# A fused attention and expert network on Trainium2: the order of projection's slots, its early loads, and the slot in which attention turns its probabilities

## The reference

```
x = x + cross_attention(layernorm(x), ctx)      # 16 heads of 32, RMS norm of q and k
x = x + expert_mlp(layernorm(x))                # 64 experts, 8 for each token
x = x + one_head_attention(layernorm(x), mem)
x = x + ternary_mlp(layernorm(x))
```

```
q = rms_norm(layernorm(x) @ Wq + bq) * wq ; k = rms_norm(ctx @ Wk + bk) * wk ; v = ctx @ Wv + bv
probs = softmax(q k^T / sqrt(32)) by head ; out = (probs @ v) @ Wo + bo
```

## Time and profile before

| | us |
|---|---|
| median of 3 runs | 1632.39 |
| the three runs | 1629.78, 1632.39, 1637.89 |
| profiled execution | 1634.27 |
| its span in the trace | 1632.5 |
| projection in it | 0 to 187.3 |
| attention | 187.3 to 385.5 |
| everything after | 385.5 to 1632.5 |

### The profile page before, as it was taken

The page is one execution under the profiler, slowest core; times in us unless marked ns, Lnnn a source line. Parts: engine busy times, 40 slices in busy tenths (PEclk is TensorE's granted clock), DMA queues, the critical chain, the costliest instruction groups (busy, mean ns, idle before and its releaser), DMA issues. The chain is left out here.

```text
span 1632.5 us, 37719 instructions
## 1 busy us (share of the span) xinstructions
PE 1441.0 (88%) x8673; PEld 1199.7 (73%) x8674; DVE 1035.1 (63%) x2067; ACT 900.0 (55%) x2048; POOL 618.4 (38%) x704
## 2 busy tenths in 40 slices
PE   6999799998954699999999999999971689999999
PEld 4777566666733588888888888888861478888888
DVE  4555467886678477777677666666635466766643
ACT  4544478885449266766666665666630234444442
POOL 0222267773132232233323233223317566666321
PEclk9999779999965799999999999999985789999999
DMA  5221493000152378778777777777638444444200
GB/s 199 78 78 60 163 367 134 2 2 30 57 225 99 111 257 289 269 265 284 257 260 257 273 252 261 252 235 260 223 100 279 145 147 126 129 133 141 77 13 28
DMA packets 94577, 278.16 MB, mean 170 GB/s; under 512 B 12901, under 2 KB 13030, under 8 KB 93798
## 3 DMA queue, kind: packets, MB, share of 16 engines
q1 hardware_dynamic: 68806, 196.00, 34.2%
q0 software_dynamic: 23680, 77.61, 15.8%
q10 hardware_dynamic: 2016, 3.67, 0.6%
HBM read 209.07 MB, written 76.81 MB: 175 GB/s over the span
## 5 line engine op out<-in xcount | busy, mean ns | idle before, releaser
L1132 POOL DMA_INDIRECT xg<-h_rows,idx x168 | 187.5, 1116 | 462.8 <-PE m_x L1160 453.3
L1175 PE MATMUL m_g<-wgu_high,bxTh 128*128 x660 | 236.0, 358 | 2.5 <-DVE bxTl L1248 2.4
L1175 PE MATMUL m_g<-wgu_low,bxTh 128*128 x660 | 223.5, 339 | 0.0
L1175 PE MATMUL m_g<-wgu_high,bxTl 128*128 x660 | 223.3, 338 | 0.0
L1578 PE MATMUL f_g<-x4T_high,ffn_gu 128*128 128x256 f32 x704 | 178.6, 295 | 12.3 <-DVE f_hid L1750 10.7
L1578 PE MATMUL f_g<-x4T_low,ffn_gu 128*128 128x256 f32 x704 | 172.1, 285 | 0.0
L1248 DVE TENSOR_TENSOR bxTl<-m_x,bxTh 128x512 fp32r<-128x512 f32 x166 | 114.7, 691 | 87.3 <-ACT bxTh L1317 78.3
L1010 DVE TENSOR_TENSOR wgu_low<-raw_gu,wgu_high x61 | 107.2, 1758 | 81.8 <-ACT wgu_high L1000 79.5
L1335 ACT ACTIVATE y<-m_y 128x512 f32<-128x512 f32 x164 | 98.2, 599 | 107.6 <-PE m_y L1195 89.2
L1469 POOL DMA_INDIRECT G<-y_rows,slot x128 | 132.8, 1037 | 56.2 <-issue 50.1
L573 POOL TENSOR_TENSOR prob<-prob,inv 128x512 f32<-128x512 f32 x128 | 130.4, 1039 | 59.7 <-DVE inv L524 59.6
(11 more groups left out here) (264 smaller groups left out, 3286.4 us busy)
## 6 DMA issues: line engine op xcount, KB each, us to landing
raw_gu<-in_exp_gu SPq DMA_DIRECT2D x64, 768.0 KB, 5.1
y_rows<-y SPq DMA_DIRECT2D x164, 256.0 KB
raw_d<-in_exp_d SPq DMA_DIRECT2D x64, 512.0 KB, 6.3
y_rows<-zero SPq DMA_DIRECT2D x64, 256.0 KB, 3.4
ffn_gu<-ffn_gu_words SPq DMA_DIRECT2D x1, 5632.0 KB, 22.2
raw_c<-in_ctxT SPq DMA_DIRECT2D x16, 256.0 KB, 2.9
X<-in_x SPq DMA_DIRECT2D x4, 1024.0 KB, 7.4
h_rows<-h SPq DMA_DIRECT2D x16, 256.0 KB, 2.0
```

Source lines behind the costliest of these rows:

```text
L1132: eng.indirect_dma_start(xg[:, u, :].bitcast(F32), None, h_dram, bass.IndirectOffsetOnAxis(ap=idx[half][:, u:u + 1], axis=0)).then_inc(s_g ...
L1175: m = eng.matmul(pg[u % 2][:, 0:2 * I], xT[l][:, u % 2, c, :], W.gu[r][:, buf * DC + c, :], start=c == 0 and n == 0, stop=c == DC - 1 and ...
```

## The change

In projection, PE's slot becomes k(s), v(s), turn_q(s-3), q(s-2), turn_k(s), and the last tiles are written out by hand: slot 15 is taken apart, so that k(15) stands between q(13) and q(14), and v(15) ahead of the last two turns. ACT and DVE get orders that match, with the next context tile in front of the k chain. At the start Wk and Wq go through SP in halves, Wv through ACT in halves, the rows in two DMAs (three and two rows at once) and one for `o_row`, which POOL alone waits for, on SP. ACT takes a root of a small tile first, and centring of Wq moves behind the first v bias. The DMAs of x tiles are issued one slot later in SP's order.

In attention, slot s-3 is turned in place of s-2, and ahead of the products; DVE copies heads 0, 1 and 3, ACT copies head 2, in the slot of its turn.

```diff
-        kn, qn, q_row, k_row = [scratch[i // 2][:, (i % 2) * D:(i % 2 + 1) * D] for i in range(4)]
-        v_row, w_row, o_row = sb("v_row", [P, D]), sb("w_row", [P, D]), spare_row
+        scratch = scratch[:, :, :].rearrange("p i (n d) -> p (i n) d", d=D)
+        kn, qn, q_row, k_row = [scratch[:, i, :] for i in range(4)]
+        two = sb("two_rows", [P, 2, D])
+        v_row, w_row, o_row = two[:, 0, :], two[:, 1, :], spare_row
...
-        s_w = [[sem(f"p_w{i}_{c}") for c in range(DC)] for i in range(3)]
+        s_w = [[sem(f"p_w{i}_{n}") for n in range(2)] for i in range(3)]
...
+            def weights(w):
+                for n in range(2):
+                    half = slice(n * DC // 2, (n + 1) * DC // 2)
+                    eng.dma_start(raw_w[:, w, half, :], wT_in[w][:, half, :]).then_inc(s_w[w][n], 16)
...
             context(0)
-            for c in range(DC):
-                eng.dma_start(raw_w[:, 2, c, :], wT_in[2][:, c, :]).then_inc(s_w[2][c], 16)
+            weights(1)
             context(1)
+            weights(0)
+            tokens(0)
             residual(0)
-            for t in tiles:
-                if t + CBUF < NT:
-                    context(t + CBUF)
-                if t % 4 == 1 and t + 3 < NT:
-                    residual(t // 4 + 1)
-                if t < NT - 1:
-                    tokens(t)
-                if t == NT - 3:
+            eng.dma_start(o_row, rows_in[5:6, :].to_broadcast([P, D])).then_inc(s_o, 16)
+            for s in tiles:
+                if s + CBUF < NT:
+                    context(s + CBUF)
+                if s % 4 == 1 and s + 3 < NT:
+                    residual(s // 4 + 1)
+                if s >= LAG:
+                    tokens(s - 1)
+                if s == NT - 2:
                     tokens(NT - 1)
...
-            for s in range(NT):
+            def mean():
+
+                eng.wait_ge(s_mean_w, 1)
+                for c in range(DC):
+                    eng.wait_ge(s_w[0][c * 2 // DC], 16)
+                    m = eng.matmul(pq[1][:, :], mean_w[:, :], raw_w[:, 0, c, :], start=c == 0, stop=c == DC - 1)
+                m.then_inc(s_mean, 1)
+                eng.wait_ge(s_id, 2)
+
+            for s in range(NT - 1):
                 k(s)
+                v(s)
+                if s == 0:
+                    mean()
                 if s >= TURN:
                     turn_q(s - TURN)
-                v(s)
-                if s == 0:
-
-                    eng.wait_ge(s_mean_w, 1)
-                    for c in range(DC):
-                        eng.wait_ge(s_w[0][c], 16)
-                        m = eng.matmul(pq[1][:, :], mean_w[:, :], raw_w[:, 0, c, :], start=c == 0, stop=c == DC - 1)
-                    m.then_inc(s_mean, 1)
-                    eng.wait_ge(s_id, 2)
-                turn_k(s)
                 if s >= LAG:
                     q(s - LAG)
+                turn_k(s)
+
+            turn_q(NT - 4)
+            q(NT - 3)
+            k(NT - 1)
             q(NT - 2)
             turn_q(NT - 3)
             q(NT - 1)
+            turn_k(NT - 1)
+            v(NT - 1)
             turn_q(NT - 2)
             turn_q(NT - 1)
...
-            for w in (1, 0):
-                for c in range(DC):
-                    eng.dma_start(raw_w[:, w, c, :], wT_in[w][:, c, :]).then_inc(s_w[w][c], 16)
-                if w == 1:
-                    for i, row in enumerate((q_row, w_row[:, :], k_row, qn, v_row[:, :], o_row)):
-                        eng.dma_start(row, rows_in[i:i + 1, :].to_broadcast([P, D])).then_inc(s_rows, 16)
+            for n in range(2):
+                half = slice(n * DC // 2, (n + 1) * DC // 2)
+                eng.dma_start(raw_w[:, 2, half, :], wT_in[2][:, half, :]).then_inc(s_w[2][n], 16)
+            for begin, rows in ((0, scratch[:, 1:4, :]), (3, two[:, :, :])):
+                end = begin + rows.shape[1]
+                eng.dma_start(rows, rows_in[begin:end, :].unsqueeze(0).to_broadcast([P, end - begin, D])).then_inc(s_rows, 16)
+
+            eng.wait_ge(s_eps, 2)
+            eng.activation(krs[:, :], eps[:, :], ACT.Sqrt)
...
+            def k_normed(t):
+                deviation(actK, t, dveK, "kb", pk[:, :], kms)
+                dveK.wait(eng, t, "kr")
+                peKT.wait(eng, t - 1, "kT")
+                actK.done(eng.activation(kn, pk[:, :], ACT.Copy, scale=krs[:, 0:1]), "kn")
...
+            for s in range(NT - 1):
+                if s > 0:
+                    k_turned(s - 1)
+                    q_root(s - TURN)
+                context(s + 1)
+                if s >= LAG:
+                k_normed(s)
+                if s >= TURN:
+                    q_turned(s - TURN)
+            k_turned(NT - 2)
+            q_root(NT - 4)
+            tokens(NT - 3)
+            q_turned(NT - 4)
+            q_root(NT - 3)
+            k_normed(NT - 1)
+            tokens(NT - 2)
+            tokens(NT - 1)
+            q_turned(NT - 3)
+            q_root(NT - 2)
+            k_turned(NT - 1)
+            q_root(NT - 1)
+            q_turned(NT - 2)
+            q_turned(NT - 1)
...
+            eng.wait_ge(s_rows, 32)
+            for s in range(NT - 1):
                 if s >= TURN:
                     q_scaled(s - TURN)
                     q_normed(s - TURN)
+                k_bias(s)
+                context(s + 1)
+                if s >= LAG:
+                    tokens(s - LAG)
+                k_scale(s)
                 if s == 0:
+                    eng.scalar_tensor_tensor(w_row, qn, -HD ** -0.5, w_row, ALU.mult, ALU.mult).then_inc(s_qw, 1)
+                if s == 1:
                     weights(0)
                     eng.wait_ge(s_qw, 1)
+                v_bias(s)
+                if s == 0:
+                    centred()
+                if s >= 1:
                     moments(s - 1)
+            q_scaled(NT - 4)
+            q_normed(NT - 4)
+            tokens(NT - 3)
+            moments(NT - 2)
+            q_scaled(NT - 3)
+            q_normed(NT - 3)
+            moments(NT - 1)
+            k_bias(NT - 1)
+            k_scale(NT - 1)
+            tokens(NT - 2)
+            tokens(NT - 1)
+            q_scaled(NT - 2)
+            q_normed(NT - 2)
+            q_scaled(NT - 1)
+            q_normed(NT - 1)
+            v_bias(NT - 1)
...
-    SLOTS, BUFS = UNITS * PAIRS, 4
+    SLOTS, BUFS, TURN = UNITS * PAIRS, 4, 3
+
+    ACT_HEAD = 2
...
+                if 0 <= s - TURN < SLOTS:
+                    turn(s - TURN)
                 if s % PAIRS == 1 and 0 <= s // PAIRS - 2 < UNITS:
                     products(s // PAIRS - 2)
-                if 0 <= s - 2 < SLOTS:
-                    turn(s - 2)
...
-                c = s - 2
+                c = s - TURN
...
-                c = s - 3
-                if 0 <= c < SLOTS and c % PAIRS == PAIRS - 1:
+                c = s - TURN
+                if 0 <= c < SLOTS and c % PAIRS == ACT_HEAD // PAIR:
                     u, x, b, g = place_of(c)
-                    peT.wait(eng, c, f"T{PAIR - 1}")
+                    peT.wait(eng, c, f"T{ACT_HEAD % PAIR}")
                     peO.wait(eng, u - 2, "O")
-                    actT.done(eng.activation(probT[:, u % 2, HG - 1, :, :], pT[PAIR - 1][:, :, :], ACT.Copy), "T3")
+                    actT.done(eng.activation(probT[:, u % 2, ACT_HEAD, :, :], pT[ACT_HEAD % PAIR][:, :, :], ACT.Copy), f"T{ACT_HEAD}")
...
-        "rows": np.stack([f["L0_xattn_" + n] for n in ("q_b", "norm_q_w", "k_img_b", "norm_k_img_w", "v_img_b", "o_b")]),
+        "rows": np.stack([f["L0_xattn_" + n] for n in ("norm_k_img_w", "q_b", "k_img_b", "v_img_b", "norm_q_w", "o_b")]),
```

More of the change, by code:

```diff
@@ L290, in _ @@
             for w in (1, 2):
-                weights(w, lambda c, w=w: eng.wait_ge(s_w[w][c], 16))
-            eng.wait_ge(s_eps, 2)
-            for s in range(NT + TURN):
-                if s >= TURN:
-                    deviation(actQ, s - TURN, dveQ, "qb", pq[(s - TURN) % 2][:, :], qms)
-                if s == NT:
-                    tokens(NT - 2)
-                    tokens(NT - 1)
-                if s >= TURN:
-                    turned(actQT, s - TURN, peQT, "qT", qT, pqT)
-                if s < NT:
-                    deviation(actK, s, dveK, "kb", pk[:, :], kms)
-                if LAG <= s < NT:
+                weights(w, lambda c, w=w: eng.wait_ge(s_w[w][c * 2 // DC], 16))
@@ L304, in _ @@
+            for s in range(NT - 1):
+                if s > 0:
+                    k_turned(s - 1)
+                if s >= TURN:
+                    q_root(s - TURN)
+                context(s + 1)
+                if s >= LAG:
                     tokens(s - LAG)
-                if s < NT:
-                    dveK.wait(eng, s, "kr")
-                    peKT.wait(eng, s - 1, "kT")
-                    actK.done(eng.activation(kn, pk[:, :], ACT.Copy, scale=krs[:, 0:1]), "kn")
+                k_normed(s)
@@ L309, in _ @@
                 if s == 0:
```

(11 more changed lines are left out.)

44 lines of the change are left out of this document (15 added, 29 removed).

## The result

| | before | after |
|---|---|---|
| median, us | 1635.14 (4 runs, 1629.78 to 1642.76) | 1610.47 (4 runs, 1608.84 to 1613.86) |
| profiled execution, us | 1634.27 | 1613.86 |
| first scores (end of projection) | 187.3 | 178.5 |
| attention, to the first matmul of the next stage | 200.1 | 181.0 |
| what follows, untouched | 1245.1 | 1252.6 |

The changed kernel takes 0.985 of the time before (95% interval 0.980 to 0.989): 24.7 us less by the medians, 20.4 between the two profiled executions. The forecast was 1604.0 with a range of 1590 to 1619. Up to the end of attention the trace shows 387.4 - 359.5 = 27.9 us saved, where the sum said 28.4. That this agrees is partly luck: projection gave half of what I expected (8.9 us for 16.4), attention over half as much again (19.1 for 12.0).

The account below looks back on a forecast made before the run. PE was taken to bound both the projection and attention loops. Gains of 7.1 + 6.0 + 3.3 + 12.0 = 28.4 us took the profiled 1634.3 to 1605.9; the median, 1.9 lower, was forecast at 1604.0 (range 1590 to 1619).

Parts of the forecast that it names:

- Start of projection: First part of projection: earlier data, no late `k(1)` and no half clock after it; gain 7.1 us (5.0 to 8.5).
- the 2.1 for the earlier data: Projection's start: Wk's second half lands at 10.6, `v(0)` starts near 15.5 in place of 17.59; gain 2.1 us.
- rival E: Projection's start bound by landing data throughout, half clocks elsewhere; at most 3 us gained there, 1626 us; chance 0.03.
- The other two terms: Projection's start: `k(1)` no longer 3.31 us late, and the half clock after it avoided, 1.6 to 1.7 us.
- The loop: Projection's slots: PE's waits for normalised q and k go, slot 9.2 us; gain 6.0 us (4 to 7).
- The tail: Projection's end, from the end of `q(12)`: 22.2 us in place of 25.5; gain 3.3 us (1 to 5).
- the clause that k(15) covers `q(14)`: Projection's tail: `k(15)` ahead of `q(14)` hides the latter's wait, so no gap was counted there.
- Attention: Attention stage: turning slot s-3 in place of s-2 makes the unit PE's 5.18 us; gain 12.0 us (6 to 14).
- rival B: Higher clock survives into attention: three units at 5.2 in place of 9.7 give 12 us more, 1592; chance 0.10.
- the 0.38 a unit for a wait for POOL: Attention's unit: PE's wait for POOL's scaling goes with the turn one slot later; 22 units x 0.38 = 8.4 us.
- C: Attention: the moved slot frees nothing, through ACT's copy ahead of the exponentials or products behind the turn; 1616 us; chance 0.15.
- D: Half clock at attention's start lasts longer, 4.5 us per extra unit; two more give 1613 us; chance 0.10.

Follow-up runs that it names:

- early_old: Changed kernel with the old early loads (four pieces per weight, 14 DMAs on ACT, six single rows, no early root); median 1611.74 us.
- tail_act: Changed kernel with x tile 14 prepared ahead of the end of k(15)'s chain on ACT and DVE; median 1594.11 us.
- turn2: Changed kernel with attention's turn put back to two slots behind the scores, not three; median 1639.51 us.
- head3: Changed kernel with ACT's copy put back to head 3, a slot after its turn; median 1654.43 us.
- proj_only: Changed projection with the attention of the kernel before; median 1615.75 us.
- warm2: Kernel tail_full plus unread transposes on PE behind projection's last turn and behind attention's second and third slots of scores; median 1585.65 us.
- tail_full: Changed kernel with projection's whole tail reordered and x tile 14 loaded early into the free context buffer; median 1590.62 us.

## Why the prediction came out as it did

**Start of projection, 7.1 expected, 5.2 found.** The mis-sized term was the 2.1 for the earlier data. I took the second half of Wk at 10.6 and `v(0)` at 15.5; ACT had it only at 11.94 and `v(0)` started at 16.93, and I priced `v(0)`'s matmuls as if they would be as fast as before from the first on (0.40), where three took 0.63. The early start is paid back in slow matmuls, and early_old shows that next to nothing is left of it: 0.5 us at the mean products against the first profile of the changed kernel, 0.1 against the second. That is what rival E said of this one term. The other two terms held. `k(1)` starts at 24.04 in place of 27.67, 3.63 us, and `k(2)` 5.16 us earlier, so the avoided half clock is 1.5 (expected 1.6 to 1.7). The rule of "DMA: Bandwidth & Descriptors" in the Trainium skill, "Issuing engines are not separate DMA queues", which I had put against this part, is in line with the two traces: ACT's freed time was worth 1.91 us at the first matmul, and nothing by the mean products.

**The loop, 6.0 expected, 7.4 found.** The slot is 9.13 us for 9.2 expected (the 9.03 in that sum adds up to 9.01), 0.53 under 9.67; from `k(3)` to `k(14)` that is 5.9 us in 11 slots. With 0.7 in the early ones and the turn of k(14), which moves into the tail, it makes 7.4. Both waits went as foreseen.

**The tail, a gain of 3.3 expected, a loss of 3.7 found.** From the end of `q(12)` (148.2) to the end of the last turn (1.39 ahead of the first scores, 177.1) it is 28.9 us, for 22.2 expected and, counted alike, 25.1 before (my 25.5 for today had six turns in it, where five follow `q(12)`). The two gaps I had in the sum came at their sizes (2.60 for 2.7, 0.91 for 1.1). The step that failed is the clause that k(15) covers `q(14)`. I compared the DMA's landing with the time k(15) gives and never followed ACT's and DVE's own order there: the new lists put tile 14 behind the chain of k(15), whose bias on DVE stands behind two other jobs. tail_act, which swaps two lines on each of these engines, gives 6.2 us back. Start, loop and tail together, 5.2 + 7.4 - 3.7, are the 8.9 us by which the first scores moved, where 16.4 were expected.

**Attention, 12.0 expected, 19.1 found.** By units of products: the 22 in the steady part give 8.5 (8.4 expected), the end 0.5 (1.0 expected). From the first scores to the eighth unit's products 10.0 us are saved where I had 2.6. Half clock at the start ends a unit's worth earlier, which is 3.6 (9.68 us in place of 6.04 for the unit after the first products) and which I had put at nothing in the forecast and at 12 in rival B. The next six take 32.1 us in place of 38.2: 2.3 of that is the same 0.39 that I counted only for 22 units, which is an omission, and 3.8 stand where I had 2.6 for POOL's work on Wo and for the fall of the clock near 229. That fall did not recur.

My reason for the gain was half of it. I took the 0.38 a unit for a wait for POOL, since the weight loads name it; but POOL had been done for 0.36 us when that load started (308.24), and what came last was ACT's copy, 0.11 us ahead of it. The size came right because the change moved the copy as well, and that is luck as far as my sum goes. I derived the unit of 5.18 from the slot distance and checked the copy's new place only as something that must fit. The timeline of before, turn2 and head3 show that it is as much a part of the gain: with three slots and the old copy the unit is 6.84. Nothing in the sum would have told the 5.17 from the 6.84, had I costed that version by "the wait for POOL goes" alone.

**Rivals.** C (nothing freed) and D (half clock longer) did not come; D was near in the profiled execution of proj_only, at 1625.81 the slowest of four (median 1615.75), where it lasted 41 us. B came in part, by one unit. What was left of it is worth 6.2 us by warm2, measured on top of the tail of tail_full.

**The total.** The sum gave 1605.9 for the profiled execution, which was 1613.86; the 8.0 us between are 7.5 in the untouched rest and 0.5 in the sum. In the second profile the rest was at its usual value, and the medians of the changed kernel were 1610.5 and 1606.7.

## What to carry to other kernels

When a hand-written order is changed, follow every engine's own queue to the moved step, not only the data and the time that the bound engine offers: the one gap that was missed stood behind two queues, and two swapped lines gave back 6.2 us. In a pipeline whose stages free each other's buffers, a longer distance and the place of a small copy are one decision; price the ring that goes through the copy before the wait that is to be removed. And TensorE's idle time costs twice: fill the gap in front of a dense stretch, if only with work that nobody reads, and see whether the clock holds.

## What the runs showed of the hardware

Half clock does not end as soon as TensorE is busy again, and how long it stays differs by the work: after a gap of 2.33 us in front of the stage behind attention, with dense matmuls of 128x512, it lasted 3.4 us (348.2 to 351.6 in tail_full), with the gap of 4.18 us ahead of `q(14)` 6.8, and at attention's start, with scores of 32 rows and transposes, 17 to 41 us. In the kernel before PE had no gap from 192.7 until the clock rose at 218.8. What sets that length I can't say from these runs.

Transposes held the clock. In warm2 28 of them in a row, 3.28 us, left it at 1.00, as did 8 ahead of the first scores and 6 behind the third slot. The Trainium skill, "TensorE: Matmul & The Clock Gate", "Part 4: PE-mode transpose", says that they don't count as busy time in the same way. These fp32 transposes gave no sign of it: the stretch that they filled is the one in which the clock otherwise fell. Whether transposes alone would also bring it back from 0.50 no run here shows.

That starting a product group earlier can be worth next to nothing, since more of the matmuls that follow then take 0.63 us in place of 0.40, was the other surprise, with 1.91 us gained at the first matmul and 0.07 left 10 us on.
